# Second wide attention: the scores of two heads in row halves of the array, and the turned weights copied by two engines

## What is computed

```python
qkv = X @ W_qkv + b_qkv                    # X is (16, 256, 128)
qkv = qkv.reshape(b, l, H, 3, D)           # H = 16, D = 64
Q, K, V = (qkv[..., 0, :], qkv[..., 1, :], qkv[..., 2, :])
scores = jnp.einsum('bqhd,bkhd->bhqk', Q, K) / D ** 0.5 + alibi    # alibi is -inf above the diagonal
weights = jax.nn.softmax(scores, axis=-1)
attn = jnp.einsum('bhqk,bkhd->bqhd', weights, V)
return attn.reshape(b, l, H * D) @ W_out + b_out
```

## Time and profile before

| | |
|---|---|
| median of 3 runs | 5003.84 us (5001.8 to 5008.87) |
| the profiled execution | 5009.49 us, its span (first to last instruction) 5007.7 us |
| mean granted TensorE clock | 0.903 |
| TensorE matmul busy, whole span | 3825.2 us (76%) |
| VectorE, ScalarE, GpSimd busy | 3459.9 us (69%), 2341.0 us (47%), 2393.5 us (48%) |

### The profile page before, as it was taken

One profiled execution on the slowest core, in us unless ns is written; L12 is line 12 of the kernel. 1 busy time (PEld: TensorE's weight loads), 2 busy tenths in 40 slices (PEclk: granted clock), 3 DMA queues, 4 the chain that ended last, 5 costly groups with the idle time before them and its releaser, 6 DMA issues. The chain is left out here.

```text
span 5007.7 us, 90777 instructions
## 1 busy us (share of the span) xinstructions
PE 3825.2 (76%) x25840; PEld 2711.9 (54%) x25840; DVE 3459.9 (69%) x9524; ACT 2341.0 (47%) x5537; POOL 2393.5 (48%) x3900
## 2 busy tenths in 40 slices
PE   5888798579999799568868936567875887699274
PEld 3666566556666466456646626422332665466264
DVE  5788676566666677556658856669998664587566
ACT  2444465256666466234446624345552553366142
POOL 3666542534444443456643344367775662232542
PEclk9999899689999899689989959889998999899597
DMA  6000232110000133133323211212221330132112
GB/s 231 1 0 0 78 123 100 45 33 1 0 0 0 54 123 109 33 122 107 106 83 121 101 36 47 72 49 64 62 62 65 118 111 23 61 122 97 38 48 81
DMA packets 243651, 341.24 MB, mean 68 GB/s; under 512 B 26848, under 2 KB 185968, under 8 KB 242224
## 3 DMA queue, kind: packets, MB, share of 16 engines
q1 hardware_dynamic: 230064, 309.19, 18.5%
q0 software_dynamic: 13184, 27.22, 1.6%
HBM read 182.77 MB, written 147.26 MB: 66 GB/s over the span
## 5 line engine op out<-in xcount | busy, mean ns | idle before, releaser
L522 DVE TENSOR_REDUCE l0att_rowmax<-l0att_S 128x2 f32<-128x512 f32 x512 | 339.3, 686 | 126.7 <-PE l0att_S L701 124.7
L892 POOL TENSOR_TENSOR wb_prob<-wb_prob,wb_rden 128x128 f32<-128x128 f32 (+1 forms) x512 | 249.0, 508 | 359.8 <-DVE wb_rden L1069 359.4
L522 DVE TENSOR_REDUCE l1ffn_rowmax<-l1ffn_S 128x2 f32<-128x512 f32 x512 | 337.4, 685 | 88.9 <-PE l1ffn_S L701 85.9
L1968 POOL TENSOR_TENSOR ssm_hc<-core_AW_all,ssm_Cs 128x512 f32<-128x512 f32 x256 | 321.2, 1271 | 130.0 <-DVE core_AW_all L2114 95.7
L1419 POOL DMA_INDIRECT results<-e_y,e_back x220 | 214.7, 976 | 291.6 <-DVE e_y L1647 259.8
L934 ACT ACTIVATE wb_prob<-wb_biased,wb_nmax 128x128 f32<-128x128 f32 (+1 forms) x512 | 228.6, 447 | 236.0 <-DVE wb_nmax L1062 233.6
L2213 PE MATMUL ssm_Y<-ssm_hc,core_ident 128*128 128x512 f32 x512 | 284.8, 665 | 57.8 <-POOL ssm_hc L1968 31.2
L2114 DVE TENSOR_TENSOR_SCAN core_AW_all<-core_AW_all,ssm_U 128x512 f32<-128x512 f32 x256 | 310.3, 1212 | 1.4 <-ACT core_AW_all L2057 1.4
L701 PE MATMUL l1ffn_S<-l1ffn_K,l1ffn_Q 128*128 128x512 f32 x512 | 249.1, 490 | 78.6 <-DVE l1ffn_rowmax L522 43.0
L1760 PE MATMUL e_H<-e_xT,e_W1s 128*128 128x128 f32 x1760 | 251.7, 287 | 72.0 <-issue 47.6
L701 PE MATMUL l0att_S<-l0att_K,l0att_Q 128*128 128x512 f32 x512 | 248.6, 489 | 61.7 <-DMA l0att_K<-bounce 48.0
(11 more groups left out here) (498 smaller groups left out, 11475.5 us busy)
## 6 DMA issues: line engine op xcount, KB each, us to landing
bounce<-l0att_parts SPq DMA_DIRECT2D x128, 256.0 KB, 2.8
bounce<-l1ffn_parts SPq DMA_DIRECT2D x128, 256.0 KB, 2.8
ssm_Cs<-c_rows SPq DMA_DIRECT2D x128, 256.0 KB, 3.1
routed<-core_Y SPq DMA_DIRECT2D x8, 2048.0 KB, 23.6
l0att_Q<-bounce SPq DMA_DIRECT2D x128, 128.0 KB
l0att_K<-bounce SPq DMA_DIRECT2D x128, 128.0 KB
bounce<-l1att_parts SPq DMA_DIRECT2D x64, 256.0 KB, 2.8
l1ffn_Q<-bounce SPq DMA_DIRECT2D x128, 128.0 KB
```

Source lines behind the costliest of these rows:

```text
L522: dve.tensor_reduce(out=rowmax[:, jp, qt, 2 * pair:2 * pair + 2], in_=S[a % 2][:].rearrange("p (j k) -> p j k", j=2)[:, :, 0:keys(qt)], op ...
L892: ins = pool.tensor_tensor(out=prob[:, w_ % 4, a:b], in0=prob[:, w_ % 4, a:b], in1=rden[:, w_ % 4, n:n + 1].to_broadcast([P, b - a]), op=A ...
L1968: pool.tensor_tensor(out=hc[:, u % 4], in0=hs[:, u % 4], in1=Cs[:, n % 4], op=ALU.mult)\
```

## The change

A joint score block, issued in even units only, makes the scores of both heads of a sequence: each of the two matmuls per head contracts over that head's 64 partitions only, alternating between heads, so that head 0 uses the upper and head 1 the lower half of the array's rows; they write to the two banks S. It waits for the maximum of the unit before, since it fills both banks. kT has one copy instead of two, needs no zeros, and its evacuation is one instruction of 128 partitions; its clearing and ScalarE's wait for it are gone. The copies of turned weights of even units (head 0) go to ScalarE, which makes them in odd units after the exponentials; those of odd units stay on VectorE, in even units.

```diff
-        kT = sb("kT", [P, SLOTS, HS, GN])
+        kT = sb("kT", [P, SLOTS, GN])
...
-            if HS == 2:
-                act.wait_ge(k_zeroed.sem, 1)
...
-                    for j in range(HS):
-                        rows = slice(j * DH, (j + 1) * DH)
-                        ins = act.activation(kT[rows, m % SLOTS, j, :], bank("k", m)[rows, :], ACT.Identity,
-                                             bias=bk[rows, m % STEPS:m % STEPS + 1])
-                    ins.then_inc(taken["k"].sem, 1)
+                    act.activation(kT[:, m % SLOTS, :], bank("k", m)[:], ACT.Identity,
+                                   bias=bk[:, m % STEPS:m % STEPS + 1]).then_inc(taken["k"].sem, 1)
...
# ScalarE's turn
-                    if merged and not (first and w_ < LAG):
+                    if (merged or (w_ - LAG) % HS == 0) and not (first and w_ < LAG):
                         copy_turned(i, w_ - LAG)
...
-            if HS == 2:
-                dve.memset(kT[:], 0.0).then_inc(k_zeroed.sem, 1)
...
# VectorE's turn
-                    if not merged and not (first and w_ < LAG):
+                    if not merged and (w_ - LAG) % HS == 1 and not (first and w_ < LAG):
                         copy_turned(i, w_ - LAG)
...
# TensorE, score
-                pe.wait_ge(maxed.sem, maxed.at(i, w_ - 1))
+                pe.wait_ge(maxed.sem, maxed.at(i, w_ + HS - 2))
                 for t, (a, b) in enumerate(parts):
-                    ins = pe.matmul(S[w_ % 2][:, a:b], qT[:, m % SLOTS, s * L + t * P:s * L + (t + 1) * P],
-                                    kT[:, m % SLOTS, j, s * L:s * L + b - a], start=True, stop=True)
-                ins.then_inc(scored.sem, 1)
+                    for h in range(HS):
+                        rows = slice(h * DH, (h + 1) * DH)
+                        ins = pe.matmul(S[(w_ + h) % 2][:, a:b],
+                                        qT[rows, m % SLOTS, s * L + t * P:s * L + (t + 1) * P],
+                                        kT[rows, m % SLOTS, s * L:s * L + b - a], start=True, stop=True)
+                        if t == QT - 1:
+                            ins.then_inc(scored.sem, 1)
...
# TensorE's turn
-                    score(i, w_)
+                    if w_ % HS == 0:
+                        score(i, w_)
```

More of the change, by code:

```diff
@@ L817, in wide_attention @@
         ready = {x: sig("ready_" + x, STEPS, 1) if rope else taken[x] for x in "qk"}
-        k_zeroed = sig("k_zeroed")
         scored = sig("scored", UNITS, SLOTS * US)
@@ L877, in rotate @@
                 pool.wait_ge(scored.sem, scored.at(i, (m + 1 - SLOTS) * US))
-                dst = qT[:, m % SLOTS, :] if x == "q" else kT[:, m % SLOTS, 0, :]
+                dst = qT[:, m % SLOTS, :] if x == "q" else kT[:, m % SLOTS, :]
                 pool.tensor_tensor(out=dst, in0=rt[:, n, 0, :], in1=rt[:, n, 1, :], op=ALU.add)\
@@ L997, in _ @@
                 for w_ in range(UNITS, UNITS + LAG + 2):
+                    if w_ < UNITS + LAG and (w_ - LAG) % HS == 0:
+                        copy_turned(TURNS - 1, w_ - LAG)
                     copy_out(TURNS - 1, w_)
@@ L1115, in _ @@
                 for w_ in range(UNITS, UNITS + LAG):
-                    copy_turned(TURNS - 1, w_ - LAG)
+                    if (w_ - LAG) % HS == 1:
+                        copy_turned(TURNS - 1, w_ - LAG)
             tail(TURNS - 1, 0)
```

## The result

The change makes the kernel slower: 5030.6 us (median of 5 runs, 5028.23 to 5032.91) against 5006.1 (5 runs, 5001.8 to 5015.1), ratio 1.0045 with an interval of 1.0033 to 1.0057. The profiled execution took 5030.15 us (span 5028.4).

The account below looks back on a forecast made before the run. Each half was taken as bound by VectorE's maximum and copy nearly as much as by TensorE. Steps +10, turn edges +5, memset -3.5, last two steps +.4 made +12 us, forecast 5016 us; stated range 4985 to 5048.

Parts of the forecast that it names:

- Parts 1 and 2: Joint score block: both heads' scores overlap in .64 us; mode switches add .09 in, .105 first load, .10 out.
- rival 1: At the joint block's edges: row halves switch free of charge, step 9.19 us, kernel 4990 us; chance .17.
- Rival 4: In the joint block: row halves don't overlap, +.63 to +1.0 us a step, kernel 5046 to 5070; chance .14.
- rival 3: In the joint block: the two halves' weight loads run in line, +.12 to .23 us a half, 5031 to 5045; chance .16.
- Part 3: New halves of a four-unit step: 4.77 and 4.80 us, step 9.57 against 9.40, put at +10 us over 64 steps.
- The near tie: Steady step before the change: TensorE reaches the second transposes (T) only .13 us after VectorE's copy allows them.
- Parts 4 to 6: Split copies, joint block's wait for the maximum, single k evacuation: each costs or gains nothing in the steady step.
- k's value of 0: One k evacuation instead of two: .7 to 1.5 us at the stage's head, set against looser first units, so 0.
- Part 7: Start of the stage: dropping kT's clearing, which ScalarE's biases and hT wait for, gives -3.5 us.
- Part 8: Turn edges, every eight steps, with residual and norm's statistics on VectorE: +.7 us a turn, +5 over seven turns.
- the likeliest case: The forecast itself: row halves overlap but pay at their edges, T waits for VectorE's copy, +12 us; chance .45.
- Rival 2: In the steady step: TensorE sets the pace, the copy being in time; step 8.75 us, kernel 4962; chance .08.

Follow-up runs that it names:

- e4: Changed kernel, but ScalarE copies odd units' turned weights at the head of even units, before the exponentials, VectorE the even units'; 4990.29 us, ratio .9961 to the kernel before.
- e5: Changed kernel with all copies of turned weights left on VectorE, so the row halves alone; 5015.77 us, ratio 1.0013 to the kernel before.
- e1: Changed kernel plus 32 dead one-column memsets of VectorE ahead of its loop over turns; 5017.69 us, ratio 1.0006 to the kernel before.
- e6: Kernel before, full-height scores and zeroed kT, with the copies split as in the change, plus 32 dead memsets; 5029.1 us, ratio 1.0043 to the kernel before.
- e9: Kernel before, full-height scores, with e8's places of copies and statistics and the 32 dead memsets; 4996.77 us, ratio .996 to the kernel before.
- e2: Changed kernel plus 96 dead one-column memsets of VectorE ahead of its loop over turns; 5040.75 us in one run.
- e3: Kernel before plus 32 dead one-column memsets of VectorE ahead of its loop over turns; 5030.14 us, ratio 1.0029 to the kernel before.
- e7: e4 plus 32 dead memsets of VectorE ahead of its loop; 4972.35 us, ratio .9923 to the kernel before.
- e8: e7 with the next norm's statistics moved from unit 8 to 13 and their application from 10 to 17; 4958.94 us, ratio .9907 to the kernel before.

## Why the prediction was right, and where it was off

**Parts 1 and 2, block and switches.** Forecast .85 to T, T .38, .99 + .09 = 1.08 from v to the joint block. Measured .86, .38 and 1.09. The load before the block starts with its matmul (both 1290.43), so it isn't hidden; its idle time behind Z is .76 and not the .17 that was named as the sign. So row halves pay at their edges as column halves do, and rival 1 (free) is out. Rival 4 (no overlap) is out by .93 for eight records, and rival 3 (loads in line) by the maximum, which starts 1.15 after the block, where the forecast had 1.155 and rival 3 .12 to .23 more. The Trainium skill ("TensorEngine Tiling (Array Packing)", Key Properties) says that a change of mode drains TensorE; these rows agree with it, for row halves too.

**Part 3, the halves.** 4.77 and 4.80 forecast, 4.77 and 4.81 read. The near tie was the right place to look, and e4 shows it from the other side: T .32 and .37 earlier gives .70 a step. One sign was hit by accident: T's waits for VectorE's copy sum to 42.6 where 45 was forecast, but the steady rows have .20 each and not .35. The rest are the five waits of about 2.4 behind the branch and those of 1.31 at the edges, so the agreement of the sums is luck. TensorE loses more than its idle bracket says (.32 and .37 by e4's starts at 2.15 and 2.10): the bracket counts from the modelled end of the matmul before, so it is safer to compare starts with starts.

**Parts 4 to 6, copies, wait, k.** Nothing in the steady step, as forecast. e5 and e1 differ by .15 a turn. k's value of 0 was right only together with the copies: once ScalarE copies, e6 shows T .27 late in its rows and a step of 9.70 instead of 9.40.

**Part 7, memset.** -3.5 forecast. From the end of the last core_X before the stage to hT it is 12.10 before (1046.13 to 1058.23) and 8.09 after (1049.33 to 1057.42): -4.0.

**Part 8, edges.** +.7 a turn forecast, +.3 measured (e1's turn less eight steps 3.44, against 3.16). ScalarE's late copies cost T .47 and .34, not .65 and .63. The forecast's 12.12, 11.11 and 3.45 can't be followed: the layout they come from isn't in its text.

**The sum, and what was missing.** From first hT to last `fin` the stage takes 634.1 before, 649.9 in e1 and 661.0 after the change. The terms for that stretch were 10 + 5 + .4 = 15.4, and e1, the change without the standstill, has +15.8: the work's own terms were right to half a microsecond in sum. Taken singly they were not, and two misses cancel: the 64 steps of .175 give 11.2 for 10, the seven edges 2.0 for 5, and the remaining 2.6, for .4, lies at the stage's two ends, where the looser start of the first units had been set against k at 0. That part of the agreement is luck. No term stood for where the code lies: 5 x 2.0 and 1.3 for the lower clock, 11.1 by the trace (661.0 - 649.9). That is most of the 14.6 by which 5016 missed; another 2.3 is the median of before, which is 5006.1 now and was 5003.84. With -4.0 at the start the stage gives +22.9, and the ratio says +22.5 (17 to 29).

So the likeliest case came true for the reason given, and the step that failed is that the sum held nothing for the code's position. That the change came out clearly slower, as the forecast had it, is owed to that and so to luck: without the standstill e1's ratio is 1.0006, +3 us (-1.5 to +8), which can't be told from no change, where its stage says +15.8 - 4.0 = +12. Those 9 us, and some 9 the other way in e9 (its stage gives -11), aren't explained by any row of the stage. The stages behind it, which no kernel changes, take between 3307 and 3320 us in the eleven profiles, 5.4 less after the change than before, and each profile is of one execution; that is wide enough to hold them, but what moves those stages wasn't settled.

The chances don't add as stated: by their parts slower is .58 and not .56, same .21, faster .21 and not .24.

**Rival 2** (8.75 a step, 4962) was given .08 and did not happen, but e4 with its step of 8.88 shows that it was one order of copies away. The prediction took the copies' places as given, rightly for this change.

## What to carry to other kernels

Before halving an engine's work, lay the chain of the next engine beside it: here the second score block lay under the wait for a copy, and halving it lost .17 us a step until the copy was moved, and gained .5 after. When a loop gets slower by an amount that no instruction accounts for, look at the first instruction behind its back-branch on each engine and at the instruction queue, and shift the code by some dead instructions before explaining anything else. Compare variants of a loop only with that standstill out of all of them: it was nearly as large here as the effect under study.

## What the runs showed of the hardware that was not expected

A loop's position can cost 2.8 us instead of .3 at a back-branch of VectorE: after, e2, e3 and e4 have it at five branches each, before, e1, e5, e6, e7, e8 and e9 at none. Five transfers of 8192 B a turn go with it, though the loop is only 333 to 364 recorded instructions long. A spell of the lower clock (.50 in e3's row) follows some of TensorE's waits of 2 us, in one to four of the five turns, and in e7 two waits of .97 and 1.30 close together. The Trainium skill ("Runtime: NRT & Kernel Launch", Instruction fetch mechanics) says that a taken branch whose target isn't in the engine's two-page window forces a fetch before execution goes on. The runs agree in kind. In size they do only in part: it names blocks of 16 KiB in a memory of 32 KiB, or 512 instructions, in which a loop of 364 would lie whole from most starts. The other instruction queue of this case, q8, moves such blocks (186 transfers of 16384 B, none in the loop), but those of q14 that come with the standstill are of 8 KiB, and a shift of 32 instructions is enough.

Two row halves of an fp32 matmul run side by side with no visible cost but their edges: eight records in .93 us, .86 to the start of T, where two full-height blocks take .65 and .66 from start to start.
